# The head-pair loop of a gram stage written out for five engines, and its gram products moved between four groups

## What is computed

```python
kv = dw3x3(einsum('oc,bchw->bohw', qkv_w, x), qkv_conv_w)      # x is group-normalised; k, v = halves
q = idwt2(dw3x3(ll, c5), dw3x3(lh, c5), dw3x3(hl, c7), dw3x3(hh, c9))   # ll, lh, hl, hh = dwt2(x)
q, k = q / norm(q), k / norm(k)                                  # per head: 8 heads of 16 channels
attn = softmax(einsum('bhdn,bhen->bhde', q, k) * temperature)
x = x + einsum('oc,bchw->bohw', proj_w, einsum('bhde,bhen->bhdn', attn, v))
```

## Time and profile before

| | |
|---|---|
| median of 3 runs | 1411.22 us (1408.17 to 1413.4) |
| profiled execution, its own time | 1407.21 us |
| its span, first to last instruction | 1405.6 us |
| busy in the span | TensorE 84%, VectorE 73%, ScalarE 63%, GpSimd 31% |
| mean granted TensorE clock | 0.934 |
| gram stage, 190 to 903 us | TensorE busy 668.2 us, VectorE 635.2, ScalarE 559.4, GpSimd 381.1 |

### The profile page before, as it was taken

How to read it: one execution, slowest core, us unless ns; L and a number is a source line. 1 busy time by engine, 2 the same in 40 slices (tenths; PEclk the granted TensorE clock), 3 DMA queues, 4 the chain that set the end, 5 groups by cost and what they waited for, 6 DMA issues and landing times. The chain is left out here.

```text
span 1405.6 us, 36822 instructions
## 1 busy us (share of the span) xinstructions
PE 1178.4 (84%) x12756; PEld 928.0 (66%) x12756; DVE 1024.2 (73%) x1771; ACT 888.6 (63%) x1574; POOL 437.9 (31%) x473
## 2 busy tenths in 40 slices
PE   0999929999999999989999999546999997999900
PEld 0555528999999899989999998323555554555500
DVE  6677418999999899989999999047766744063394
ACT  0677837888888788878888886010443354766383
POOL 6100024556555555545556553120000010000010
PEclk9999959999999999999999999768999999999955
DMA  9976792534544534544535540358877330000079
GB/s 329 417 305 266 312 187 73 137 97 127 136 119 115 145 96 129 140 114 109 144 94 132 143 111 35 102 199 301 277 249 246 101 118 1 0 1 0 0 287 401
DMA packets 148705, 221.26 MB, mean 157 GB/s; under 512 B 115625, under 2 KB 116789, under 8 KB 144193
## 3 DMA queue, kind: packets, MB, share of 16 engines
q1 hardware_dynamic: 137456, 152.26, 35.8%
q0 software_dynamic: 6480, 47.19, 8.9%
q10 hardware_dynamic: 4608, 19.67, 4.0%
HBM read 131.84 MB, written 87.20 MB: 156 GB/s over the span
## 5 line engine op out<-in xcount | busy, mean ns | idle before, releaser
L1675 PE MATMUL b_conv_bank<-b_sign,wsign 128*128 (+1 forms) x1728 | 296.7, 329 | 10.5 <-ACT b_sign L1455 7.9
L1675 PEld LDWEIGHTS b_conv_bank<-b_sign,wsign 128*128 128x128 bf16 x1728 | 168.6, 98 | 141.0 <-issue 28.7
L756 POOL TENSOR_TENSOR b_vacc<-b_vacc 128x576 f32<-128x576 f32 x128 | 180.4, 1409 | 210.1 <-ACT b_vacc L850 209.3
L989 PE MATMUL b_bank<-b_tkh,b_kt 96*96 96x100 f16 x1536 | 222.3, 210 | 2.3 <-DVE b_tml L970 2.3
L990 PE MATMUL b_bank<-b_tkl,b_kt 96*96 96x100 f16 x1536 | 222.0, 210 | 0.0
L991 PE MATMUL b_bank<-b_tkh,b_kt 96*96 96x100 f16 x1536 | 222.0, 210 | 0.0
L989 PE MATMUL b_bank<-b_yh,b_tmh 96*96 96x200 f16 x768 | 195.1, 254 | 21.2 <-DVE b_tml L954 6.4
L947 DVE SCALAR_TENSOR_TENSOR b_value_sum<-b_vin,b_vtaps,b_value_sum 128x576 f32<-128x576 f32 x256 | 206.6, 807 | 0.0
L1474 ACT CAST b_y<-b_conv_bank 128x384 f32 (+1 forms) x192 | 91.2, 478 | 171.1 <-PE b_conv_bank L1675 169.2
L989 PEld LDWEIGHTS b_bank<-b_tkh,b_kt 96*96 96x96 f16 x1536 | 194.1, 126 | 3.7 <-DVE b_tml L970 2.5
L991 PEld LDWEIGHTS b_bank<-b_tkh,b_kt 96*96 96x96 f16 x1536 | 194.2, 126 | 0.0
(11 more groups left out here) (214 smaller groups left out, 2554.3 us busy)
## 6 DMA issues: line engine op xcount, KB each, us to landing
b_vin<-value_projection_scratch SPq DMA_DIRECT2D x32, 686.0 KB, 5.9
value_projection_scratch<-b_vout ACTq DMA_DIRECT2D x24, 784.0 KB, 4.6
keys_scratch<-b_khl SPq DMA_DIRECT2D x24, 784.0 KB, 3.5
b_kt<-keys_scratch SPq DMA_DIRECT2D x128, 147.0 KB, 2.9
b_xraw<-in_x SPq DMA_DIRECT2D x128, 144.0 KB, 5.1
values_scratch<-b_vacc SPq DMA_DIRECT2D x32, 576.0 KB, 3.3
b_values<-values_scratch SPq DMA_DIRECT2D x48, 384.0 KB, 3.9
out<-xs SPq DMA_DIRECT2D x25, 576.0 KB, 7.0
```

Source lines behind the costliest of these rows:

```text
L756: nc.gpsimd.tensor_tensor(whole, whole, room, ALU.add).then_inc(s_padd, 1)
L989: nc.tensor.matmul(out, w_hi, m_hi, start=first, stop=False)
L1675: ins = nc.tensor.matmul(cbank[k % NBK][:, 0:CH].rearrange("p (r c) -> p r c", c=W), p["wsign"][nth // NIMG][:, t * C:(t + 1) * C], padded ...
```

## The change

All five `with ....Fori(0, LOOPS) as hh:` become `for hh in range(LOOPS):`, so the loop is written out when the program is built: three copies of the eight groups on each engine, constants in place of registers, no branch. And the table of pieces is another one; its sums, 50 and 50, and the points of the copies and of the null products are the same. The whole diff:

```diff
@@ -655,7 +655,7 @@
 
             for i in range(PEEL):
                 body(i, i, (i + 2) // (NG // NIMG), True)
-            with sp.Fori(0, LOOPS) as hh:
+            for hh in range(LOOPS):
                 for k in range(PAIR):
                     if k == GPH:
                         store_gram(hh * 2)
@@ -779,7 +779,7 @@
                 add_product(0, 0, 0, n)
             for i in range(PEEL):
                 body(i, i, MID)
-            with pool.Fori(0, LOOPS) as hh:
+            for hh in range(LOOPS):
                 for k in range(PAIR):
                     body(PEEL + k, hh * PAIR + (PEEL + k), MID, hh * 2 + k // GPH)
             for i in range(NG - GPH, NG):
@@ -815,7 +815,7 @@
                     b[0:W, 0:nb * n * wide].rearrange("p (b m o) -> p b m o", b=nb, m=n))
 
         units = [[(2 * e + im, blk) for im in range(2) for blk in range(S2B // RUN)] for e in range(GPARTS - 1)]
-        PIECES = [{0: 7, 1: 7, 2: 7, 3: 7, 4: 11, 5: 11}, {6: 3, 7: 3, 8: 7, 9: 7, 10: 7, 11: 7, 12: 16}]
+        PIECES = [{0: 9, 1: 9, 2: 9, 3: 8, 4: 8, 5: 7}, {6: 4, 7: 7, 8: 7, 9: 7, 10: 7, 11: 9, 12: 9}]
         COPY_AT, NULL_AT = [6, 13, 14], 13
         assert all(sum(counts.values()) == len(unit) for counts, unit in zip(PIECES, units))
 
@@ -912,7 +912,7 @@
             level(act, s_hi)
             for i in range(1, PEEL):
                 body(i, i, 0, MID)
-            with act.Fori(0, LOOPS) as hh:
+            for hh in range(LOOPS):
                 for k in range(PAIR):
                     body(PEEL + k, hh * PAIR + (PEEL + k), hh * (PAIR // 2), MID, hh * 2 + k // GPH)
             for i in range(NG - GPH, NG):
@@ -972,7 +972,7 @@
             level(dve, s_dve)
             for i in range(1, PEEL):
                 body(i, i, 0, MID)
-            with dve.Fori(0, LOOPS) as hh:
+            for hh in range(LOOPS):
                 for k in range(PAIR):
                     body(PEEL + k, hh * PAIR + (PEEL + k), hh * (PAIR // 2), MID)
             for i in range(NG - GPH, NG):
@@ -1113,7 +1113,7 @@
             level(pe, s_pe)
             for i in range(1, PEEL):
                 body(i, i, 0, MID)
-            with pe.Fori(0, LOOPS) as hh:
+            for hh in range(LOOPS):
                 for k in range(PAIR):
                     body(PEEL + k, hh * PAIR + (PEEL + k), hh * (PAIR // 2), MID, hh * 2 + k // GPH)
             for i in range(NG - GPH, NG):
```

## The result

| | median | runs | |
|---|---|---|---|
| kernel before | 1410.72 us | 4, 1408.17 to 1413.4 | |
| changed kernel | 1395.15 us | 4, 1390.65 to 1398.04 | ratio 0.9886, 95% interval 0.9861 to 0.9912 |

The ratio stands for a gain of 16.1 us (12.4 to 19.6). The forecast of 1397.8 us, a gain of 13.4, lies inside the interval and 2.6 us above the median. The profiled execution took 1390.65 us, the fastest of the four, with a span of 1389.0 us.

A forecast was written before the change was run, and what follows sets the result against it. The prediction took VectorE's beat of 20.44 us a group as the gram stage's bound. Jumps 8.6 plus products 4.8 make 13.4 us off the 1411.2 us median: 1397.8 us, range 1392.1 to 1404.1 us.

The forecast's parts named there:

- The jumps, 8.60 us: Gram stage loop: writing it out removes two jumps back, with TensorE's branch stall and half clock, 3.56 + 5.04 us.
- ScalarE's and VectorE's covered stalls: Loop head: gaps of 4.1 and 2.9 us after their branches, hidden by TensorE's stall, next in line if it alone went.
- The Trainium skill's 108 ns: Documented compare-and-branch cost: TensorE's two loop jumps would cost 0.2 us, their removal nothing; the prediction rejected it.
- The products, 0.68 us a head: Moving gram products off crowded rows wins 0.47 us in fourth and 0.21 us in second groups, 4.8 us over seven heads.
- the residue of 0.05 us: Fourth group of a head: the forecast won back only 0.47 of its 0.52 us lag behind the beat.
- the 5.0: Limit on the moved products' gain in us: over 0.72 us a head was held excluded by VectorE's beat.
- Rows of nine products cost nothing: New table's rows with 9 gram products, not in the earlier trace: taken at nothing, bounded at 0.6 us in all.
- Straight code costs nothing: Code of 16 added groups and dropped register steps: costed at nothing, as straight groups were as long as loop groups.
- The beat as VectorE's: Gram stage: undisturbed groups take 20.44 us, set by VectorE's work, with TensorE a few tenths under it.
- Rival 1: ScalarE's 1.07 us copy, not the products' places, makes second and fourth groups long; only jumps won, 1402.6 us, chance 0.13.
- Rivals 2 and 3: Stall reappears in straight code or branch was worth little, 1406.4 us, chance 0.03; last-stage loop jumps dearer, 1415.0 us, chance 0.02.
- rival 3: Last stage: longer TensorE code makes small loops' jumps cost about 4.3 us instead of 0.21, 1415.0 us, chance 0.02.

The follow-up runs named there:

- e1: Changed kernel (loop written out on all five engines) with the old table of gram product pieces: 1400.51 us, ratio 0.9925.
- e2: Kernel before, loop kept on all five engines, with only the new table of gram product pieces: 1403.64 us, ratio 0.9964.
- e4: Changed kernel with the loop kept on TensorE alone, written out on the other four engines: 1403.2 us, ratio 0.9952.
- e3: Kernel before with the new table and the loop written out on TensorE alone, kept on the other four engines: 1400.37 us, ratio 0.9931.
- e7: Changed kernel with one of a group's twelve value taps moved from VectorE to a ScalarE product and a GpSimd addition: 1402.59 us, ratio 0.9941.
- e8: e7 with ScalarE's first tap of the second half, normalisations and first high copy of x moved to earlier places: 1390.26 us, ratio 0.9837.
- e6: e1 with ScalarE copying only an eighth of the gram bank from the second head on (result not computed): 1394.5 us, ratio 0.9899.
- The repeated run: The changed kernel unaltered, measured again beside the other experiments on the same chip: 1396.2 us, ratio 0.9898.
- e10: e8 with the fourth group's gram bank copy one row later and the null products moved too: 1384.26 us, ratio 0.9816.
- e5: e2 with a back-edge hint on each engine's loop: 1400.05 us, ratio 0.9921.

## Why the prediction was right

- **The jumps, 8.60 us.** Right in kind, and in size for the execution it was read from. Straight code without them (e1) is 7.96 us shorter over the 27 groups, 8.7 with the 0.7 us that the 12 crowded groups gained in length. But a jump scatters: e2 and e4 paid 7.2 to 7.8 us for the same two. That the forecast took the sum of one cheap and one dear jump off a median, and came so near, is in part luck; the range allowed for it.
- **ScalarE's and VectorE's covered stalls.** The step that they would be next in line if TensorE's loop alone were written out is shown by e3: 1.5 us a jump. Which of the two decides was left open; it is VectorE, whose gap is the shorter but whose branch comes later. The reading that these gaps "end about when TensorE's first result is there" was loose. In the trace of before ScalarE's gaps end at 461.2 and 629.9 us, and its next copy, of TensorE's first result, starts at 462.81 and 632.23: the stalls were covered with 1.6 and 2.3 us to spare.
- **The Trainium skill's 108 ns** (Advanced Engine Details and Errata, Control Flow Timing) would have left only the 4.8 us of the products. The branches of L1116 in e2 and e4 (3482 to 3988 ns) and the time of e1 contradict it for a loop of this length.
- **The products, 0.68 us a head.** In the loop the second group gave 20.65 - 20.43 = 0.22 us and the fourth 20.95 - 20.42 = 0.53 us (e2), 0.07 us more a head than forecast: the residue of 0.05 us that the forecast left in the fourth group is not there in the loop. In straight code it is 20.71 - 20.42 = 0.29 and 21.02 - 20.45 = 0.57 us (e1 against the changed kernel). Of the seven heads six stood in the loop of the kernel before, so this part brought 6 x 0.75 + 0.86 = 5.4 us in place of 4.8, slightly over the 5.0 that the prediction called excluded.
- **Rows of nine products cost nothing.** Right: the first group, 0,9,9,9, takes 20.44 us.
- **Straight code costs nothing.** Right for groups at the beat to a hundredth of a microsecond; for crowded ones it cost 0.06 us, which group 29 of the kernel before, straight code, already has: 20.72 us where the second groups in the loop have 20.65. Why is not known.
- **The beat as VectorE's.** The prediction took 20.44 us for a bound by VectorE's work. No term hung on more than that undisturbed groups take this long, and that held in all 27. The name of the bound did not: with 1.2 us less work on VectorE the group took 20.54 us (e7) and, with ScalarE's work in another order, 20.15 us (e8); with a shorter copy on ScalarE and all of VectorE's work fourth groups took 20.32 us (e6). This fits a chain through both engines, in which VectorE's waits for ScalarE's high copies count beside its work; the chain itself was not taken apart.
- **Rival 1** had half of the truth. e6 shows that shortening the copy is as good a cure as moving the products; the forecast had rested on ScalarE's idle time ahead of the copy, and that reading held.
- **Rivals 2 and 3** did not come. No gap of TensorE turned up in the straight code: its longest wait between 300 and 800 us is 0.7 us. The time behind the 27 groups is 2 us shorter in one profile of the changed kernel and 2 us longer in the other, so nothing of the size of rival 3 is there, and no branch of L1681, L1688 and L1697 takes over 0.24 us in either.
- **The 2.6 us beyond the forecast** are inside the measurement's interval; the stage itself gave 13.17 + 0.57 = 13.7 us against the 13.4 forecast. The jumps gave a little less and the products a little more than their terms. The repeated run has 1396.2 us.

## What to carry to other kernels

Where a group of work takes its shortest time in some places and longer in others, price a jump, a crowded row or a copy as the difference of two groups of one trace; here that held to 0.1 us where the cost did not itself scatter. Before an engine's stall is removed, look at what the others do under its cover: in a loop each engine jumps for itself, and here writing out TensorE's alone left 3 us of 7. Whether GpSimd's and SyncE's loops had to be written out too was not tried. The busiest engine need not be the bound: a product moved from VectorE to the less busy ScalarE made the group longer (e7). Spare time counts only where it lies: that product fitted ScalarE's average and not its fullest stretch, and moving a copy by one row was worth 3 us in the 27 groups (547.26 in e8, 544.31 in e10).

## What the runs showed of the hardware

- A taken branch at the end of a long loop (about 5100 products and weight loads of TensorE a round: 8600 + 8599 in 27 groups, eight groups a round) held TensorE's sequencer for 3.5 to 4.2 us in all six jumps profiled without a hint; in the small loops of the last stage it took 0.21 us.
- On ScalarE and VectorE the branch itself is recorded with 45 to 63 ns, and the stall of 3.5 to 4.1 and 2.8 to 3.0 us shows only as silence of the sequencer up to the loop's first instruction (before, e2, e3). On GpSimd and SyncE this gap was 0.3 us (before and e2).
- A hint at the loop's head shortened the stall to 2.1 us on TensorE and 0.5 us on ScalarE, and on VectorE to no less than 2.7 us (e5).
- After 2.9 and 3.5 us of idle time TensorE ran at a granted clock of about a half; after 0.7 us of it at most, in e3, it stayed at 1.00. In e5 both came of nearly the same idle time: after 1.50 us the clock stayed at 1.00 at the first jump, and after 1.55 us at the second it fell to half 0.8 us after TensorE had started again (0.68 on average from 624.4 to 628.0 us).
